# A two-layer graph kernel with a 32 KB instead of a 16 KB scratch for the descriptors of dynamic DMAs

## What is computed

```
# layer 0: 4 heads of 32
m = x @ W_n2m.T;  q, k, v = m @ Wq.T + bq, m @ Wk.T + bk, m @ Wv.T + bv
e = (edge_attr @ W_edge.T) @ We.T
alpha = softmax over the edges of one dst of  (q[dst] * (k[src] + e)) summed per head, scaled
out   = sum over the edges of one dst of  (v[src] + e) * alpha
beta  = sigmoid([out, x_r, out - x_r] @ Wbeta.T)       # x_r = m @ Wskip.T + bskip
x     = layernorm(x + (beta * x_r + (1 - beta) * out) @ W_m2n.T)
# layer 1: one head of 256
scores = q[dst] . k[src] * scale + edge_weight * we + be, softmax over the edges of one dst
out    = sum of v[src] * attn;  layer norm, FFN with gelu, layer norm, layer norm
```

## Time and profile before

| | |
|---|---|
| median of 3 runs | 5680.19 us |
| the profiled execution | 5642.29 us |
| its span, first to last instruction | 5640.5 us |
| busy: PE, DVE, POOL, ACT | 71%, 77%, 66%, 31% of the span |
| DMA queue of POOL's gathers | 169,040 packets, 436.01 MB |
| mean granted clock of TensorE | 0.857 |

### The profile page before, as it was taken

How to read it: one execution, slowest core, us unless ns; L and a number is a source line. 1 busy time by engine, 2 the same in 40 slices (tenths; PEclk the granted TensorE clock), 3 DMA queues, 4 the chain that set the end, 5 groups by cost and what they waited for, 6 DMA issues and landing times.

```text
span 5640.5 us, 109399 instructions
## 1 busy us (share of the span) xinstructions
PE 3987.2 (71%) x27082; PEld 3334.8 (59%) x27082; DVE 4361.3 (77%) x15007; ACT 1731.9 (31%) x4312; POOL 3738.7 (66%) x3955
## 2 busy tenths in 40 slices
PE   6566667666666666666667777777777777777887
PEld 3466566566666566664455655556566555655676
DVE  5677778777778777878867777777777777777798
ACT  0366666666666666662200000000000000000222
POOL 0577777777777777751177777777777777776354
PEclk9788788888788888879978898888888898888999
DMA  5777777777877777853377777777777777776222
GB/s 152 195 210 205 209 209 207 211 207 204 213 209 208 210 209 207 214 154 109 109 198 202 197 197 189 195 198 198 200 197 200 196 198 199 197 195 178 68 73 65
DMA packets 847299, 1042.01 MB, mean 185 GB/s; under 512 B 286127, under 2 KB 598400, under 8 KB 846736
## 3 DMA queue, kind: packets, MB, share of 16 engines
q1 hardware_dynamic: 536000, 501.80, 34.5%
q0 software_dynamic: 169040, 436.01, 28.9%
q10 hardware_dynamic: 141696, 97.92, 5.6%
HBM read 931.22 MB, written 129.77 MB: 188 GB/s over the span
## 4 chain that ended last, share of the span: by engine, by line
issue 27%; POOL 27%; DMA 20%; DVE 15%; PE 6%; DVEq 4%; POOLq 1%; ACT 0%; SPq 0%; ACTq 0%
POOL rows L581 27%; DMA rows<-kv_d,idx 10%; DMA rows<-x_d,idx 8%; PE ps L1276 5%; DVEq L330 2%; DMA acc_d<-acc 2%; DVE prod L926 2%; DVE oh L1057 1%; DVE acc L1077 1%; DVE oht L894 1%; DVE rows L1175 1%; DMA idx<-idx_d 1%; DVE nq L858 1%; DVE rows L854 1%; DVEq L1133 1%
## 5 line engine op out<-in xcount | busy, mean ns | idle before, releaser
L581 POOL DMA_INDIRECT rows<-kv_d,idx x1760 | 1723.6, 979 | 752.7 <-issue 538.5
L581 POOL DMA_INDIRECT rows<-x_d,idx x1760 | 1779.5, 1011 | 612.4 <-issue 541.7
L1276 PE MATMUL ps<-qw,oht 128*128 128x128 bf16 (+2 forms) x12320 | 1228.9, 253 | 26.9 <-DVE oht L894 26.3
L1276 PEld LDWEIGHTS ps<-qw,oht 128*128 128x128 bf16 x12320 | 1044.4, 107 | 234.2 <-issue 41.4
L1276 PE MATMUL ps<-rows,oh 128*128 128x257 f32 x3520 | 1006.4, 441 | 185.5 <-DVE oh L1057 146.0
L926 DVE CUSTOM_DVE_ANT_0 prod<-rows,ps 128x256 f32<-128x256 f32 x1760 | 636.5, 417 | 422.0 <-DMA rows<-x_d,idx 313.7
L1276 PEld LDWEIGHTS ps<-rows,oh 128*128 128x128 f32 x3520 | 739.7, 218 | 319.6 <-DVE oh L1057 200.2
L903 DVE TENSOR_TENSOR rows<-rows,ps 128x1024 f32<-128x1024 f32 x440 | 535.8, 1218 | 375.4 <-DMA rows<-kv_d,idx 360.2
L1276 PE MATMUL ps<-msg,oh 128*128 128x132 f32 x3520 | 564.8, 313 | 337.4 <-DVE msg L1052 168.2
L1276 PEld LDWEIGHTS ps<-msg,oh 128*128 128x128 f32 x3520 | 495.6, 216 | 379.3 <-DVE msg L1052 363.9
L700 ACT ACTIVATE pen_r<-ps 128x128 f32<-128x128 f32 (+1 forms) x110 | 29.9, 272 | 2207.1 <-PE ps L1356 2207.1
(11 more groups left out here) (201 smaller groups left out, 4480.6 us busy)
## 6 DMA issues: line engine op xcount, KB each, us to landing
dst_row<-in_dst_row SPq DMA_DIRECT2D x880, 256.0 KB
qw<-q_d SPq DMA_DIRECT2D x440, 192.8 KB
acc_d<-acc ACTq DMA_DIRECT2D x440, 128.5 KB
ea<-in_eaT SPq DMA_DIRECT2D x440, 128.0 KB
qw<-q_d SPq DMA_DIRECT2D x440, 96.0 KB
acc_d<-acc ACTq DMA_DIRECT2D x440, 66.0 KB
rows<-kv_d,idx POOLq DMA_INDIRECT x1760
rows<-x_d,idx POOLq DMA_INDIRECT x1760
```

The lines of the kernel that those rows point to most:

```text
L581: pool.indirect_dma_start(out=L.rows[par][:, st, j, 0:D], out_offset=None, in_=L.table, in_offset=bass.IndirectOffsetOnAxis(ap=idx[par][:, ...
L1276: return pe.matmul(out_, lhsT=lhsT, rhs=rhs, start=first, stop=last)
```

## The change

The scratch is given as 32,768 bytes. To make room, begun lies in the first 7040 bytes of oh's space and stepped in those of msg's, since neither is read once the prologue is over. No instruction is added, removed or moved, and no wait is added. [...]

```diff
-        begun = sb("begun", [P, SG, NPAIR])
-        stepped = sb("stepped", [P, SG, NPAIR])
...
-        oh = sb("oh", [P, OHS, JT, P])
+        oh_space = sb("oh", [P, OHS * JT * P])
+        oh = oh_space[:, :].rearrange("p (s j n) -> p s j n", s=OHS, j=JT)
+        begun = oh_space[:, 0:SG * NPAIR].rearrange("p (g n) -> p g n", g=SG)
...
-        msg = [sb(f"msg{b}", [P, JT, DM + HEADS]) for b in range(OHS)]
+        msg_space = sb("msg", [P, OHS * JT * (DM + HEADS)])
+        msg = [msg_space[:, b * JT * (DM + HEADS):(b + 1) * JT * (DM + HEADS)].rearrange("p (j n) -> p j n", j=JT)
+               for b in range(OHS)]
+        stepped = msg_space[:, 0:SG * NPAIR].rearrange("p (g n) -> p g n", g=SG)
...
-    nc = bacc.Bacc("TRN2", target_bir_lowering=False, num_devices=1)
+    nc = bacc.Bacc("TRN2", target_bir_lowering=False, num_devices=1, dynamic_dma_scratch_size=32768)
```

## The result

The changed kernel takes 5636.07 us in the median of five runs (5610.85 to 5649.53); the kernel before 5680.19 us, also of five (5672.07 to 5692.97). The ratio is 0.9925, with a 95% interval of 0.9903 to 0.9947: 0.75% faster. The forecast was 0.14% faster, in a range of 5628 to 5695 us.

The account below looks back on a forecast made before the run. POOL's stream of 3520 gathers was taken to bound the kernel. Fewer long gaps gave 8 us, gathers, tables and addresses 0: 5680.2 - 8 = 5672 us, 0.14% down, range 5628 to 5695 us.

Parts of the forecast that it names:

- the rival of 7 gaps: POOL's long gaps: scratch size is the only limit, 7 gaps in a layer, about 5635 us; chance 0.20.
- the forecast's own case: POOL's long gaps: 13 or so in a layer instead of 15, at today's prices, 8 us gained; chance 0.62.
- POOL's stream bounds the kernel, and what leaves its idle time leaves the kernel: Edge stages, 84% of the time: 3520 gathers set the pace; idle time removed shortens the kernel, up to POOL's waits for consumers.
- The long gaps are room running out: POOL's gaps after 113, then every 112 gathers: room for its writes runs out; 15 a layer, 91.1 us in all.
- A second limit at 128: POOL's open DMAs: gaps ahead of the 129th gather, then every 127 or 128; 13 in a layer instead of 15.
- The price of a gap: POOL's long gaps: each lasts until outstanding transfers land; 2.61 and 3.47 us apiece beyond 0.30, varying with place in the chunk.
- positions 1 and 17: Places in a 32-gather chunk where gaps alternate: 3.02 and 4.36 us at 1, 2.82 and 3.24 us at 17.
- 2 x 2.61 + 2 x 3.47: Both edge layers: two gaps fewer in each at mean price, saving 12.2 us; 8 us taken, between 3.0 and 12.2.
- Each gather itself: POOL's gathers: same descriptors in a larger ring, 0 change, bound 6 ns each, 21 us either way over 3520.
- Saved gaps come back: POOL's other idle time: with four gaps fewer, at most 4 x 0.49 = 2 us return as other waits.
- Tables and addresses at 0: begun and stepped sharing room, and shifted buffer addresses: 0, the addresses within the gathers' bound of 21 us.
- The slower rival: Gaps at the chunk's head, fewer but dearer: 5717 us; chance 0.07 of being slower by more than 0.5%.

Follow-up runs that it names:

- the copy: The kernel before run once more with no edit, on one chip in one session with the change: ratio 1.0005 to the kernel before.
- the pair: The kernel before and the changed kernel, both unedited, run once more on one chip in one session: ratios 1.0005 and 0.9932.
- the pad: Against the change: no scratch size given (16 KB as before), and an unused tile of 16,384 bytes ahead of the other tiles: ratio 1.0002.

## Why the forecast was right in part

The direction was right and the size was not: 8 us (0.14%) were forecast, 44 us (0.75%) measured. 5636.07 us lies in the range only because its lower end had been drawn down to take in the rival of 7 gaps; the forecast's own case spanned 5655 to 5692 us, and a gain of more than 28 us had a chance of 0.24.

- **POOL's stream bounds the kernel, and what leaves its idle time leaves the kernel.** Right: 34.1 us of idle and 16.0 us of busy time gone from POOL account for the 49.8 us gone from the edge stages. Between the medians of the copy and the change lie 40 us.
- **The long gaps are room running out, counted in gathers of one size, emptied by the drain at a stage's end.** Right: the count follows the size at eight sizes that were given, and it begins anew in layer 1 at each. The traces also bracket what a gather takes: a 113th doesn't fit in 16,256 bytes and 124 fit in 17,920, so it is between 143.9 and 144.5 bytes (16,256 / 113 and 17,920 / 124), by my estimate 144. 4096, 8192, 8320, 8448, 8576, 12,160, 16,256 and 17,920 divided by 144 are 28, 56, 57, 58, 59, 84, 112 and 124 whole gathers, and each trace agrees. The kernel before names no size; at 144 bytes a gather its room for 113 is from 16,272 to 16,415 bytes, and 16,384 lies in that.
- **A second limit at 128.** Supposed, and measured: 128, then 124 apart. Why it should be 128 no run shows: it was my guess, and it came true; nor does any show what the limit counts (in bytes it would be 128 x 144 = 18,432 by the estimate above). The rival with 7 gaps, in which the size is the only limit, is refuted, though it named 5635 us and the median came to 5636: the right time for a wrong reason. The prediction had 13 gaps; it is 14, since four gathers stay on account.
- **The price of a gap.** This step failed. The prediction priced the gaps by their place in the chunk (positions 1 and 17) and said that a wait is "for the outstanding transfers to land", so that its length is "not the number of entries cleared". It is for all but those of the step begun last, and the place that matters is that in the step: positions 1 and 17 are both a step's second gather, and steps of 128, which the prediction put at the dear price of position 1, lead to a step's first. The entries cleared count as well, 0.0234 us each at that place. Nor does POOL go on at the landing: it is 1.80 us later in the kernel before. The term "2 x 2.61 + 2 x 3.47", cut to 8 us, measured 36.5 us: 28 waits at 1.77 us instead of 30 at 2.87 us. The trace before had the signs of that rule: 113 less 112 is the one gather spared, 113 is one more than 28 steps, and the 1.80 us stand behind the landing of the step before at all 30 waits.
- **Each gather itself.** Put at 0 within 21 us either way. The queue of the gathers carries the same 169,040 packets and 436.01 MB before and after; POOL's busy time was 16.0 us lower in the pair. Between executions of kernels with 16 KB it lies from 1717.1 to 1724.4 us in layer 0, with 32 KB it is 1710.7 and 1720.0; some of the 16 us may be the change's, and no run separates it.
- **Saved gaps come back.** At most 2 us by the prediction; 2.4 us in the pair. In the first profile of the change the forced waits cost 60.1 us and the other gaps above 0.30 us 83.2 us, against 91.1 and 46.4 us before, and nothing was gained in it; that one execution is the slowest of its five.
- **Tables and addresses at 0.** Right: 1.0002 with the pad and the shared tables. That tiles lie elsewhere in the change follows from the sizes alone; no trace shows an address.
- **The slower rival** (each wait dearer at the chunk's head) didn't come about: the 28 waits average 1.77 us beyond 0.30, and it needed 3.50.

## What to carry to other kernels

When a POOL stream of indirect DMAs sets the pace, count the gathers between its unexplained gaps: first count and later distance give the room and, by their difference, how many gathers a wait leaves in flight. Choose the scratch so that the room is a whole number of the groups that the program itself waits for; one gather more or less was worth 1.2 to 2.3%, doubling the scratch 0.7%. Here 16,256, 8192 or 4096 bytes (0.988, 0.990, 0.988) beat both kernels with less room than either, and need no shared tables to fit. This holds where POOL's stream sets the pace: on the chip where POOL waited for its consumers, 8192 bytes in the old kernel and 12,160 in the changed one took 0.6% and 0.5% more than the kernel before.

## What the runs showed of the hardware

- The room steps with the size of the scratch, by one gather for about 144 bytes (estimate from 16,256 bytes with 112 and 17,920 with 124), and the time can step with it: 8192 bytes 56 gathers and 0.9902, 8320 bytes 57 and 1.0132.
- Beside the room there is a limit of 128 gathers on account (32,768 bytes: 128, then 124), be it one of gathers or of bytes.
- A forced wait spares the gathers of the step begun last, 1, 2, 3 or 4 of them. A step's four gathers share one semaphore here, and neighbouring steps use different ones; whether that is what groups them wasn't tried.
- Behind the landing that it asks for, a forced wait takes a constant time that grows with the gathers cleared: at a step's first gather 0.66 us for 24 to 3.00 us for 124 more than without one, at the second 1.15 us for 56 and 1.80 for 112. Where the landing lies far enough ahead it adds no idle time (108 to clear, 3.41 us of delay, landing 3.50 us ahead, 0.30 us idle at 608.36).
- One chip ran the same kernel in 7118 us, where others took 5643 to 5680, at a granted clock of 0.78 instead of 0.86.
